# Node products of the message stage: two lumps per epoch, or six pieces between the message pairs

## What is computed

```python
s1 = jnp.einsum('ea,eb,abc->ec', xs, es, W1) * (1.0 / np.sqrt(MUL0_N * MUL0_E))
s2 = jnp.einsum('eai,ebi,abc->ec', xv, ev, W2) * (1.0 / (np.sqrt(3.0) * np.sqrt(MUL1_N * MUL1_E)))
...
v1 = jnp.einsum('ea,ebi,abc->eci', xs, ev, W3) * (1.0 / np.sqrt(MUL0_N * MUL1_E))
v2 = jnp.einsum('eai,eb,abc->eci', xv, es, W4) * (1.0 / np.sqrt(MUL1_N * MUL0_E))
...
row, col = (edge_index[0], edge_index[1])
tp = fctp_messages(node_features[col], edge_attr_tensor, W1, W2, W3, W4)
messages = tp @ Wm + bm
agg = jax.ops.segment_sum(messages, row, num_segments=N_NODES)
```

## Time and profile before

| | us |
|---|---|
| median of three runs (5759.46 to 5767.8) | 5759.57 |
| the profiled execution | 5760.69 |
| its span, first to last instruction | 5758.9 |
| of it the message stage, from the second epoch's first scatter to the last but one's (171.8 to 2491.6) | 2319.8 |
| the second layer's stage and what ends it (3000 to 5759) | 2759 |

### The profile page before, as it was taken

One profiled execution on the slowest core, in us unless ns is written; L12 is line 12 of the kernel. 1 busy time (PEld: TensorE's weight loads), 2 busy tenths in 40 slices (PEclk: granted clock), 3 DMA queues, 4 the chain that ended last, 5 costly groups with the idle time before them and its releaser, 6 DMA issues. The chain is left out here.

```text
span 5758.9 us, 109402 instructions
## 1 busy us (share of the span) xinstructions
PE 4257.5 (74%) x31805; PEld 3204.8 (56%) x31805; DVE 3701.5 (64%) x7179; ACT 1385.8 (24%) x3804; POOL 3186.2 (55%) x3214
## 2 busy tenths in 40 slices
PE   4777777777777777769997676777767767776766
PEld 3555555555555555559996454545444445545444
DVE  8776667677767665558884555555555555555555
ACT  3433333333333333310003111111111111111111
POOL 1666666666666666650003566656665565555654
PEclk9877777887777777779998777777777777777777
DMA  7444444444444444449992222222222222222222
GB/s 167 110 110 113 110 112 113 113 110 109 112 112 112 113 111 111 113 145 303 302 289 78 58 59 59 59 59 60 59 59 59 59 58 59 59 57 58 60 59 42
DMA packets 605069, 591.90 MB, mean 103 GB/s; under 512 B 183845, under 2 KB 486662, under 8 KB 604662
## 3 DMA queue, kind: packets, MB, share of 16 engines
q1 hardware_dynamic: 420070, 256.17, 18.6%
q0 software_dynamic: 151488, 262.69, 17.0%
q10 hardware_dynamic: 33424, 72.03, 3.8%
HBM read 431.87 MB, written 158.72 MB: 103 GB/s over the span
## 5 line engine op out<-in xcount | busy, mean ns | idle before, releaser
L2995 POOL DMA_INDIRECT q_fg<-f,q_index x1568 | 1552.0, 990 | 1039.8 <-issue 484.1
L1141 POOL DMA_INDIRECT messages<-stage,place x1568 | 1572.7, 1003 | 884.4 <-issue 507.4
L1445 PE MATMUL ps_m<-by_attr,turned 128*128 128x160 f32 x6272 | 1163.1, 340 | 239.2 <-issue 231.4
L1445 PEld LDWEIGHTS ps_m<-by_attr,turned 128*128 128x128 f32 x6272 | 1057.9, 217 | 387.2 <-issue 378.2
L3249 PE MATMUL q_ps_m<-q_prod,q_onehot_sh 128*32 128x160 f32 x12544 | 824.2, 375 | 361.7 <-issue 217.8
L3057 DVE SCALAR_TENSOR_TENSOR q_sums<-q_ps_m,split_q,q_sums 128x161 f32 x784 | 301.6, 385 | 1041.0 <-issue 935.9
L1223 DVE SCALAR_TENSOR_TENSOR turned<-rel_row,quarter,flipped 128x512 f32<-128x512 uint8 x784 | 528.2, 746 | 637.8 <-remote 542.8
L3249 PEld LDWEIGHTS q_ps_m<-q_prod,q_onehot_sh 128*32 128x32 f32 x12544 | 485.3, 133 | 621.2 <-issue 391.3
L3236 PE MATMUL q_ps_w<-q_wfc,q_hidden 64*128 64x192 f32 x3136 | 615.4, 435 | 253.6 <-issue 237.3
L3236 PEld LDWEIGHTS q_ps_w<-q_wfc,q_hidden 64*128 64x128 f32 x3136 | 381.8, 237 | 397.7 <-issue 354.0
L1366 ACT COPY stage<-ps_m 128x320 f32<-128x320 f32 x784 | 317.0, 437 | 1112.8 <-remote 818.0
(11 more groups left out here) (282 smaller groups left out, 4248.9 us busy)
## 6 DMA issues: line engine op xcount, KB each, us to landing
nat<-in_edge_attr SPq DMA_DIRECT2D x392, 256.0 KB
rows_in<-messages ACTq DMA_DIRECT2D x208, 324.0 KB, 3.4
rows_in<-messages SPq DMA_DIRECT2D x208, 324.0 KB, 3.4
rel_row<-rel_rows SPq DMA_DIRECT2D x98, 256.0 KB
messages<-stage,place POOLq DMA_INDIRECT x1568
q_fg<-f,q_index POOLq DMA_INDIRECT x1568
q_a<-in_edge_attr SPq DMA_DIRECT2D x196, 64.0 KB
messages<-zeros SPq DMA_DIRECT2D x31, 324.0 KB, 8.0
```

Of the source, the lines that this page charges most:

```text
L1141: nc.gpsimd.indirect_dma_start(out=msgs, out_offset=bass.IndirectOffsetOnAxis(ap=place[:, r, k:k + 1], axis=0), in_=stage[:, r, k, :], in_ ...
L1445: last = nc.tensor.matmul(ps_m[g % BANKS][:, k % 2 * D0:k % 2 * D0 + D0], turned[:, r, half, k * P:(k + 1) * P], by_attr[:, r, k, :, half] ...
L2995: nc.gpsimd.indirect_dma_start(out=fg[:, i, place_of(v), :], out_offset=None, in_=f_tab, in_offset=bass.IndirectOffsetOnAxis(ap=index[:, i ...
```

## The change

The eight matmuls of the node products are put into six pieces: three of one matmul that were `products_a`, then XZ alone, then XX with XS, then XY with XS. Piece 0 stands behind message pair 1, piece 5 behind pair 6, so pair 7 is the last work of an epoch. Each piece raises `s_y` by itself (six per epoch, `YPS`, in place of two), and waits for ACT: pieces 0 to 2 for the turned features, piece 3 to 5 for ACT's copy of piece 0 to 2, whose banks they reuse. On ACT the copies of piece p stand behind the copy of message pair p+2. The number of matmuls, their shapes, banks, factors and the twelve steps of `s_ev` are the same. The first two epochs' products, which are made in the part ahead of the stage, go by the same helpers.

```diff
-            def products_a(banks):
-                product(banks[0], 0, XS, W12, xt, w_xy)
-                product(banks[1], 0, XX, W12, xt, w_xy)
-                return product(banks[2], 0, XY, W12, xt, w_xy)
-
-            def products_bc(banks):
-                product(banks[0], 0, XZ, W12, xz, w_z)
-                product(banks[1], 0, XX, W34, xt, w_xy)
+            YPS = 6
+
+            def node_product(banks, piece):
+                if piece == 0:
+                    return product(banks[0], 0, XS, W12, xt, w_xy)
...
+                if piece == 4:
+                    product(banks[1], 0, XX, W34, xt, w_xy)
+                    return product(banks[1], 256, XS, W34, xt, w_xy)
                 product(banks[2], 0, XY, W34, xt, w_xy)
-                product(banks[1], 256, XS, W34, xt, w_xy)
                 return product(banks[2], 256, XS, W34, xz, w_z)
+
+            def node_step(pe, n, piece, banks):
+                pe.wait_ge(s_ev, n * YEV + max(2, piece))
+                node_product(banks, piece).then_inc(s_y, 1)
...
+            def keep_piece(act, n, r, piece, banks):
+                act.wait_ge(s_y, n * YPS + (piece + 1))
...
-                            for g in range(4):
+                            for g in range(PAIRS0):
                                 message(n, r, g, not last)
-                            if span:
-                                find(t + 1, r, *span)
-                            if not last:
-                                keep_a(n + 2, r)
-                            for g in range(4, PAIRS0):
-                                message(n, r, g, not last)
-                            if not last:
-                                keep_bc(n + 2, r)
+                                if g == 3 and span:
+                                    find(t + 1, r, *span)
+                                if g == 2 and not last:
+                                    act.wait_ge(s_attr, n * 3 + 3)
+                                if g >= 2 and not last:
+                                    keep_piece(act, n + 2, r, g - 2, ps_y)
...
                         def epoch(t, r, ahead=True):
                             n = t * 2 + r
-                            for g in range(4):
+                            for g in range(PAIRS0):
                                 messages(t, r, g, ahead)
-                            if ahead:
-                                step_a(n + 2)
-                            for g in range(4, PAIRS0):
-                                messages(t, r, g, ahead)
-                            if ahead:
-                                step_bc(n + 2)
+                                if ahead and 1 <= g <= YPS:
+                                    node_step(pe, n + 2, g - 1, ps_y)
```

More of the change, by code:

```diff
@@ L699, in product @@
                                         tile_position=(rows.start, 0))
-            def products_a(banks):
-                product(banks[0], 0, XS, W12, xt, w_xy)
-                product(banks[1], 0, XX, W12, xt, w_xy)
-                return product(banks[2], 0, XY, W12, xt, w_xy)
-            def products_bc(banks):
-                product(banks[0], 0, XZ, W12, xz, w_z)
-                product(banks[1], 0, XX, W34, xt, w_xy)
+            YPS = 6
+            def node_product(banks, piece):
+                if piece == 0:
+                    return product(banks[0], 0, XS, W12, xt, w_xy)
+                if piece == 1:
+                    return product(banks[1], 0, XX, W12, xt, w_xy)
+                if piece == 2:
+                    return product(banks[2], 0, XY, W12, xt, w_xy)
+                if piece == 3:
+                    return product(banks[0], 0, XZ, W12, xz, w_z)
+                if piece == 4:
+                    product(banks[1], 0, XX, W34, xt, w_xy)
+                    return product(banks[1], 256, XS, W34, xt, w_xy)
@@ L721, in keep_rest @@
-            def keep_rest(r, banks):
-                keep(r, banks[0], 0, 512, S_, BZ, F2)
-                keep(r, banks[1], 0, 256, X_, BS, F4)
-                keep(r, banks[2], 0, 256, Y_, BS, F4)
-                keep(r, banks[1], 256, 256, X_, BX, F3)
-                keep(r, banks[1], 256, 256, Y_, BY, F3)
-                keep(r, banks[1], 256, 256, Z_, BZ, F3)
-                keep(r, banks[2], 256, 256, Z_, BS, F4)
+            def keep_piece(act, n, r, piece, banks):
+                act.wait_ge(s_y, n * YPS + (piece + 1))
+                if piece == 0:
+                    keep(r, banks[0], 0, 512, S_, BS, F1)
+                elif piece == 1:
+                    keep(r, banks[1], 0, 512, S_, BX, F2)
+                elif piece == 2:
+                    keep(r, banks[2], 0, 512, S_, BY, F2)
+                elif piece == 3:
+                    keep(r, banks[0], 0, 512, S_, BZ, F2)
+                elif piece == 4:
+                    keep(r, banks[1], 0, 256, X_, BS, F4)
+                    keep(r, banks[1], 256, 256, X_, BX, F3)
+                    keep(r, banks[1], 256, 256, Y_, BY, F3)
+                    keep(r, banks[1], 256, 256, Z_, BZ, F3)
+                else:
+                    keep(r, banks[2], 0, 256, Y_, BS, F4)
+                    keep(r, banks[2], 256, 256, Z_, BS, F4)
@@ L983, in _ @@
                             turned_nodes(r)
-                            act.wait_ge(s_y, 2 * r + 1)
                             act.wait_ge(s_blank_y, r + 1)
-                            keep_first(r, head_y)
-                            act.wait_ge(s_y, 2 * r + 2)
-                            keep_rest(r, head_y)
+                            for piece in range(YPS):
+                                keep_piece(act, r, r, piece, head_y)
                             find(4 + r)
@@ L1043, in _ @@
                             nc.tensor.matmul(ps_v[0:NV, P:2 * P], xw[:, r, P:D0], sel[:, r, :], start=True, stop=True).then_inc(s_xt_ps, 1)
-                            pe.wait_ge(s_ev, r * YEV + 2)
-                            products_a(head_y).then_inc(s_y, 1)
-                            pe.wait_ge(s_ev, r * YEV + 5)
-                            products_bc(head_y).then_inc(s_y, 1)
+                            for piece in range(YPS):
+                                node_step(pe, r, piece, head_y)
                         for c in range(1, SPANS):
@@ L1423, in turn_xz @@
                             nc.tensor.matmul(ps_xz, xw[:, r, P:D0], sel[:, r, :], start=True, stop=True).then_inc(s_xt_ps, 1)
-                        def step_a(n):
-                            pe.wait_ge(s_ev, n * YEV + 2)
-                            products_a(ps_y).then_inc(s_y, 1)
-                        def step_bc(n):
-                            pe.wait_ge(s_ev, n * YEV + 5)
-                            products_bc(ps_y).then_inc(s_y, 1)
                         def messages(t, r, g, ahead):
```

11 lines of the change are left out of this document (removed).

## The result

The changed kernel takes 5984.2 us (median of 4 runs, 5974.8 to 6004.3) against 5759.5 us of the kernel before beside it: a ratio of 1.040, interval 1.037 to 1.043. It is slower by 225 us, where 114 were forecast.

The account below looks back on a forecast made before the run. POOL's 16 transfers plus one wait were taken to bound the 24.40 us epoch; 24.76 + 0.4 + 0.4 = 25.6 us, 1.2 more over 95 epochs, gave about 5874 us, range 5700 to 6130.

Parts of the forecast that it names:

- The ring: POOL's epoch in the message stage: 19.6 us to the 16th transfer's start, then 3.3, then restart 1.2; 24.12 us.
- the release: Moment when PE's held signals come together, 3.3 us behind the start of POOL's last transfer in an epoch.
- PE's sum: PE's work per epoch at full clock: from 14.35 to 17.7 us, or 18.2 if products sharing a bank don't overlap.
- The one term taken in the middle: PE, pieces 4 and 5: lost overlap of 32-row and 64-row products, nothing or +1.05 us; +0.5 taken.
- no row of before shows it either way: Claim that the earlier profile doesn't show whether the products in pieces 4 and 5 overlap; 0.5 or 1.05 us.
- The short wait becomes the rule: Fourth pair at 10.3 us behind POOL's start makes POOL pause ahead of its ninth transfer; ordinary epoch 24.76 us.
- The share of caught handshakes: Epochs where piece 5 and pair 7 wait for ACT's copy of piece 2: one in ten, 0.4 us on average.
- Rival (a): Every epoch pays 3.3 to 5.3 us for the handshake ahead of pair 7: 29.0 us an epoch, 6200 us; chance 0.10.
- The slow epochs: Closing caveat: PE's slow stretch may begin elsewhere once its stream is mixed; no size given.
- The wait of piece 0: PE behind pair 1 waits for ACT's copy of the turned features: 0.5 us, bounds 0.3 and 2.
- (b): Faster: last pair signalled before POOL's 16th transfer, so POOL never runs dry; 5712 us, or 5637 if nearly all; chance 0.18.
- (c): No change: PE's extra 3.4 us fit under POOL's time; 5760 us, at most 10 away; chance 0.10.

Follow-up runs that it names:

- e7: Changed kernel with POOL's middle stop moved from its ninth to its 13th transfer, asking for pair 4 instead of pair 3; 1.039 of the kernel before.
- e8: Changed kernel with piece 0 behind pair 2, pieces 1 and 2 behind pair 3, the rest behind pair 7; 1.002 of the kernel before (4849 us chip).
- e4: Changed kernel with pieces 3, 4 and 5 all behind pair 7 on PE and ACT; 1.012 of the kernel before.
- e5: Changed kernel with pieces 0 to 2 in one row behind pair 3, their copies ahead of pair 4's; 1.009 of the kernel before.
- e1: Changed kernel with ACT's copy of piece 2 ahead of pair 4's copy instead of behind it; 1.017 of the kernel before.
- e9b: Kernel before with the second row of products ahead of pair 7 and ACT's copies of the first row behind pair 4's copy; 1.022 of the kernel before.
- c3: The changed kernel again, unaltered, on a chip where the kernel before takes 4848 us; 1.118 of the kernel before.

## Why the prediction missed, step by step

**The ring** held: the release comes 3.3 us behind POOL's last transfer, and a last pair behind it is paid in full. e7 shows the cause.

**PE's sum** held. Each of pieces 0 to 3 with its pair takes 2.38 us (1437.14 to 1439.52), as 1.05 and 1.12 + 0.21 say. The one term taken in the middle was at its far end: the two products of piece 4 take 1.25 us to the next pair (1446.66 to 1447.91), not 0.53. With it the sum comes to 18.1 us: 3.07 for turns and two pairs, 0.34 of wait, four times 2.38 and twice 2.58. By Gotcha 1 (PSUM pressure) of the Trainium skill's page "TensorEngine Tiling (Array Packing)" the estimate was 18.2, and the trace agrees with the number. It does not show that the shared bank is the reason. In e8, where pieces 3 to 5 run in a row, a product of 64 rows (1393.65) and the next one of 32 rows (1394.27, among the same four records) write different banks, and they don't overlap either; the last one starts at 1394.90:

```profile
1393.65 1.32 PE L698 MATMUL ps_y<-w_xy,xt 64*128 64x256 f32 x4
1394.90 0.70 PE L698 MATMUL ps_y<-w_z,xz 64*128 64x256 f32 x2
```

The kernel before had shown as much: XS, of 64 rows, goes alone for 1.05 us ahead of XX and XY, which write two other banks. So "no row of before shows it either way" was wrong, and the prediction's own rows pointed to 1.05 for the term.

**"The short wait becomes the rule"** was wrong: POOL's 16th transfer came later than 20.5 us in 25 of 95 epochs, in 38 before, and POOL paused ahead of its ninth transfer (over 0.5 us) in 12, in 26 before. The fourth pair came 8.3 us behind POOL's start on average, not 10.3. The early half alone does bring the wait (53 in e4), the late half alone does not (14 in e5). So the pause that I counted on, to let pair 4's signal through, got rarer.

**The share of caught handshakes** is the term that was mis-sized. The chain itself (pair 4, copy of piece 2, piece 5, pair 7) was the right one, and so was its price, 3.3 to 5.3 us: 28.40 against 24.81 are 3.6. But I put it at one epoch in ten, 0.4 us on average, and it is 38 in 95, and 47 and 48 in the two repeats: 1.6 to 1.8 us. Undoing it alone (e1) gives back some 1.1 to 1.5, making it alone (e9b) costs 0.9 to 1.3. The earlier trace rows had shown pair 4's signal held in an ordinary epoch; I set that against a pause that another step of the same sum had to deliver. Rival (a) was right in mechanism and nearly in its 29 us, for two epochs in five, half in the repeats. What decides which epoch is caught is open: in some, as above, PE starts early behind a caught one and is free, but 12 of the 38 stand directly behind another.

**The slow epochs** stood only in the last sentence of the prediction. They add 0.8 us in the first profile (77 us in 95 epochs), 0.4 to 0.5 in the repeats. The prediction had half clock for 6 us behind a release and no longer; the runs show stretches of 26 to 32 us in these epochs. The sum has no term for that.

**The wait of piece 0** was right on the chip of the measurement (0.34 us, forecast 0.5) and wrong in its bounds: "0.3 to 2" took ACT to be busy with the release, and not to wait for its stage buffer, which gave 5.9 us on the other kind of chip.

**Rivals (b) and (c)**: no row of short epochs came. The sum of what was measured apart on the slow-signal chips, 0.77 early half, 0.43 late last pair, 1.32 chain, is 2.5 us of 2.2 to 2.6 over three profiles; by the ratios it is 0.7, 0.4 or 0.5, and 0.9, together 2.1 of 2.3 to 2.4. That they simply add up was not tested by itself.

## What to carry to other kernels

Before a lump is cut up and spread between the steps of a critical stream, ask of each piece which signal its input or its buffer waits for, and whether that signal is one that the trace shows held: a handshake that was free behind the last step is paid in full ahead of it. Where a forecast rests on how often an epoch falls into one of two patterns, count how the trace of before divides and ask what feeds the next epoch; don't take a small share because another term makes room for it. And look at what the granted clock did behind each idle stretch: here the stream with four pairs in a row had it back within 12 us after 53 gaps of 53, and the stream with a product after every pair after 3 of 43.

## What the hardware showed unexpectedly

The same kernel runs at 5750 to 5860 us in some groups and at 4850 us in others. On the first kind of chip PE's signals and its matmuls (one every 2 to 2.8 us) are held while POOL issues indirect transfers back to back, and come 3.3 us behind the last one; on the second ACT has no wait of that kind, and an epoch is POOL's own 21 us. The same change costs 4.0% on one and 11.8% on the other, most of it by different mechanisms. The experiments that ran on the second kind alone said next to nothing of the first.

PE's granted clock stayed at 0.50 for 28 us with PE busy in every slice, where products and pairs alternated (c3, 1400 to 1428), and was back at 1.00 at most 12 us behind the gap where pairs stood in a row (e8). A product of 64 rows and one of 32 did not overlap, in one PSUM bank (1.25 us together) or in two, while two of 32 rows in two banks did (1.06 us together in the earlier trace rows).
